# Cross-attention on one core: the query projection and the output projection change places within a TensorE step

## The reference, cut to what is computed

```python
q = split_heads(x @ Wq.T, 20)                 # x: 2 x 2048 x 640, 20 heads of 32
k = split_heads(ctx @ Wk.T, 20)               # ctx: 2 x 77 x 1024
v = split_heads(ctx @ Wv.T, 20)
probs = softmax(einsum('bhsd,bhld->bhsl', q, k) / sqrt(32), axis=-1)
out = merge_heads(einsum('bhsl,bhld->bhsd', probs, v))
return out @ Wo.T + bo + x
```

## Time and profile before

| | us |
|---|---|
| median of 3 runs | 434.07 (433.29 to 434.44) |
| the profiled execution | 434.35 |
| its span, first to last instruction | 432.6 |
| PE busy in it | 424.6 (98%) |
| ACT, POOL, DVE busy in it | 253.9, 301.0, 231.6 |

### The profile page before, as it was taken

The page is one execution under the profiler, slowest core; times in us unless marked ns, Lnnn a source line. Parts: engine busy times, 40 slices in busy tenths (PEclk is TensorE's granted clock), DMA queues, the critical chain, the costliest instruction groups (busy, mean ns, idle before and its releaser), DMA issues.

```text
span 432.6 us, 8258 instructions
## 1 busy us (share of the span) xinstructions
PE 424.6 (98%) x2538; PEld 310.7 (72%) x2538; DVE 231.6 (54%) x437; ACT 253.9 (59%) x509; POOL 301.0 (70%) x256
## 2 busy tenths in 40 slices
PE   8999989999999999999999999999999999999996
PEld 6877765577776777777777677777777767777775
DVE  0354785655555555555555555555555555555623
ACT  1638887757465755748464755757564755755510
POOL 8337798999658765969659674969659684865460
PEclk9999999999999999999999999999999999999999
DMA  8998536444454346543455335643355333444203
GB/s 280 353 327 266 210 110 220 150 149 145 137 197 157 134 156 204 192 146 125 145 184 184 124 131 205 205 168 124 124 192 192 128 122 137 156 159 161 76 24 121
DMA packets 39614, 72.68 MB, mean 168 GB/s; under 512 B 5024, under 2 KB 6176, under 8 KB 39584
## 3 DMA queue, kind: packets, MB, share of 16 engines
q1 hardware_dynamic: 28784, 52.62, 34.6%
q10 hardware_dynamic: 10800, 19.67, 14.1%
HBM read 28.81 MB, written 10.49 MB: 91 GB/s over the span
## 4 chain that ended last, share of the span: by engine, by line
PE 89%; DMA 3%; SPq 2%; ACT 2%; POOL 1%; DVE 1%; issue 1%; POOLq 0%; ACTq 0%
PE ps_q L672 30%; PE ps_o L672 27%; PE ps_s L734 10%; PE ps_pv L741 7%; PE ps_m L720 5%; PE ps_den L746 4%; PE ps_o L655 2%; DMA x_f<-in_x 2%; PE ps_m L787 1%; DMA q_packed<-mxT 1%; PE ps_m L725 1%; PE ps_q L787 1%; SPq L264 1%; DVE x_f L576 1%; PE ps_o L787 1%
## 5 line engine op out<-in xcount | busy, mean ns | idle before, releaser
L336 POOL TENSOR_TENSOR p_lo<-p_f,p_hi 77x512 f16<-77x512 f32 x160 | 183.9, 1168 | 99.7 <-ACT p_hi L430 97.3
L426 ACT ACTIVATE p_f<-ps_s 77x512 f32<-77x512 f32 x160 | 94.7, 592 | 45.7 <-PE ps_s L734 45.7
L546 DVE TENSOR_REDUCE mx<-ps_m 128x4 f32<-128x308 f32 x160 | 69.3, 475 | 54.8 <-PE ps_m L720 54.6
L430 ACT ACTIVATE p_hi<-ps_s 77x512 f16<-77x512 f32 x160 | 93.5, 584 | 2.8 <-PE ps_den L746 2.7
L539 DVE TENSOR_TENSOR q_lo<-ps_q,q_hi 128x512 fp32r<-128x512 f32 x40 | 27.7, 692 | 102.6 <-ACT q_hi L412 102.6
L672 PE MATMUL ps_q<-x_hi,wq_hi 128*128 128x512 f32 x200 | 79.5, 397 | 0.7 <-POOL x_lo L327 0.3
L672 PE MATMUL ps_q<-x_lo,wq_hi 128*128 128x512 f32 x200 | 78.2, 391 | 0.0
L672 PE MATMUL ps_q<-x_hi,wq_lo 128*128 128x512 f32 x200 | 78.2, 391 | 0.0
L672 PE MATMUL ps_o<-attn_hi,wo_hi 128*128 128x512 f32 x170 | 69.7, 410 | 0.6 <-POOL attn_lo L342 0.6
L672 PE MATMUL ps_o<-attn_hi,wo_lo 128*128 128x512 f32 x170 | 66.9, 393 | 0.0
L672 PE MATMUL ps_o<-attn_lo,wo_hi 128*128 128x512 f32 x170 | 66.8, 393 | 0.0
(11 more groups left out here) (105 smaller groups left out, 517.1 us busy)
## 6 DMA issues: line engine op xcount, KB each, us to landing
q_packed<-q_hi SPq DMA_DIRECT2D x80, 256.0 KB, 2.5
x_f<-in_x SPq DMA_DIRECT2D x40, 256.0 KB, 3.4
q_packed<-q_lo SPq DMA_DIRECT2D x40, 256.0 KB, 3.2
x_res<-in_x ACTq DMA_DIRECT2D x35, 256.0 KB, 2.7
out<-out_sb ACTq DMA_DIRECT2D x35, 256.0 KB, 2.6
wk_sb<-in_wk SPq DMA_DIRECT2D x8, 320.0 KB, 5.8
wv_sb<-in_wv SPq DMA_DIRECT2D x5, 512.0 KB, 5.9
wq_sb<-in_wq SPq DMA_DIRECT2D x5, 320.0 KB, 4.8
```

What stands on the lines that cost most here:

```text
L336: nc.gpsimd.tensor_tensor(p_lo[:, i, :], p_f[:, i, :], p_hi[:, i, :], ALU.subtract).then_inc(plo_done, 1)
L426: nc.scalar.activation(p_f[:, i, :], ps_s[i % 2][0:L, :], ACT.Exp, scale=SCALE).then_inc(pf_done, 1)
L430: nc.scalar.activation(p_hi[:, i, :], ps_s[i % 2][0:L, :], ACT.Exp, scale=SCALE).then_inc(phi_done, 1)
L546: nc.vector.tensor_reduce(mx[:, g % RS, :, tt], ps_m[tt % 2][:, 0:HG * L].rearrange("p (h k) -> p h k", k=L), AX_X, ALU.max).then_inc(max_ ...
```

## The change

In PE's steps the two projections change places: the query projection goes chunk by chunk into the places between maxima and scores, the output projection runs whole at the end. In steps that have no query projection left, (7, 3) and (7, 4), the output projection stays in the places. The filling steps are untouched, so 32 steps change, (1, 1) to (7, 2). On DVE q_low is issued ahead of finish_out. No instruction is added or removed.

```diff
@@ DVE, step
+                if exists(shift(t, g, 2)[0]):
+                    q_low(*shift(t, g, 2))
                 for tile in out_tiles(t, g):
                     finish_out(*tile)
-                if exists(shift(t, g, 2)[0]):
-                    q_low(*shift(t, g, 2))
@@ PE, step
-                if tiles:
-                    project_out(*tiles[0], (0, 1))
+                query = shift(t, g, 2)
+
+                def between(chunks):
+                    if exists(query[0]):
+                        project_q(*query, chunks)
+                    elif tiles:
+                        project_out(*tiles[0], chunks)
+
+                between((0, 1))
                 if exists(max_t):
                     max_scores(max_t, max_g, 2, batch(max_t))
                     max_scores(max_t, max_g, 3, batch(max_t))
                 if exists(t):
                     scores(t, g, 2, batch(t))
-                if tiles:
-                    project_out(*tiles[0], (2, 3))
+                between((2, 3))
                 if exists(t):
                     scores(t, g, 3, batch(t))
                 if exists(max_t):
                     transpose_max(max_t, max_g)
-                if tiles:
-                    project_out(*tiles[0], (4,))
-                if exists(shift(t, g, 2)[0]):
-                    project_q(*shift(t, g, 2), range(G))
+                between((4,))
+                if exists(query[0]) and tiles:
+                    project_out(*tiles[0], range(G))
```

## The result

The changed kernel takes 448.07 us (447.43 to 448.49, 4 runs) against 433.68 us before (433.10 to 434.44, 4 runs): ratio 1.0332, 95% interval 1.0316 to 1.0347. That is 14.4 us more; 15.3 were predicted, with 444.4 to 454.5 as the range.

The account below looks back on a forecast made before the run. PE's own instructions were taken to bound the kernel from step (1, 2) on. The profiled 434.35 us plus 15.8 (six blocks, 2.63 each) less 0.5 for step (1, 1) gave 449.6 us, range 444.4 to 454.5.

Parts of the forecast that it names:

- Steady steps cost nothing: In steady steps the swapped projections, new waits, DVE's order and transfers were to cost nothing.
- The transfers' collision: Rival: pack_q's transfer stretches load_max past 4.8 us, scores 0 wait 0.5 us in 32 steps, 466 us; chance 0.03.
- ACT's casts wait for output tile (t-2, 4): Steps (t, 0), t = 2 to 7: attn_high of chunks 0 and 1 waits until that tile has read them.
- Exponentials 2 3.77 us late: ACT in step (t, 0): exponentials 2 start 3.77 us late behind the waiting cast, and everything behind is as late.
- place 1: Start of step (t, 1): PE's `values` wait for ACT's last p_hi, 1.15 us late.
- place 2: Step (t, 1): the second part of `values` waits for POOL's last p_lo, 1.73 us late.
- place 3: Step (t, 1): scores 0 wait for load_max, the query projection for q_low, up to 1.9 us late.
- place 4: Step (t, 2): the second part of `values` waits for POOL's gapless attn_low and p_low chain, 2.63 us late in all.
- Step (1, 1) gains 0.5: Output projection no longer waits for attn_lo, about 1.2 us; a new p_lo wait leaves 0.5, bounds 0 and -1.8.
- the rival: Clock falls after PE's pauses: six steps take double, 509 us; chance 0.02.
- Only step (t, 1) pays: Rival: POOL has more room, only step (t, 1)'s waits remain, 1.7 to 1.9 us a block, 444.5 us; chance 0.06.
- Not slower: Rival: attn_high's wait in step (t, 0) is covered, only step (1, 1)'s gain remains, about 433.3 us; chance 0.03.

Follow-up runs that it names:

- experiment 1: Changed kernel with PE's and DVE's old order put back in the steps with g = 0 alone; 432.94 us, ratio 0.9994 to the kernel before.
- experiment 3: Changed kernel with ACT's five attn_high casts put last in its steps with g = 0, PE and DVE untouched; 433.17 us, ratio 1.0006.
- experiment 4: Changed kernel with POOL's attn_low of chunks 3 and 4 in blocks 1 to 6 cut to 64 of 512 columns; 444.46 us, ratio 1.0247.
- experiment 6: Changed kernel with five extra 16-column subtractions on POOL ahead of attn_low of chunk 4, blocks 1 to 6; 457.54 us, ratio 1.0517.
- experiment 7: As experiment 3, plus in step (1, 0) attn_high 0 and 1, q_high, attn_high 2 to 4, all behind exponentials 3; 432.28 us, ratio 0.9965.
- experiment 9: Kernel before the change with only experiment 7's new order in ACT's step (1, 0); 432.67 us, ratio 0.9985.
- experiment 10: The version of experiment 7 run once more, on the same chip as experiment 9; 432.26 us, ratio 0.9973.
- experiment 2: Changed kernel with the swap kept only in the steps with g = 0, all others as before; 452.52 us, ratio 1.0431.
- experiment 5: Changed kernel with DVE's old order, finish_out ahead of q_low, and PE as changed; 448.00 us, ratio 1.0332.
- experiment 8: As experiment 2 (swap only in steps with g = 0), but finish_out ahead of q_low everywhere; 451.20 us, ratio 1.0401.

## Why the prediction was right, point by point

- *Steady steps cost nothing.* Shown by experiment 1: of its 26 swapped steps none after (1, 2) is over 9.86 us. The transfers' collision did not come; load_max of the changed kernel landed after 1.8 to 4.3 us, below the 4.84 from which it would have counted:

```profile
DMA to landing us min/median/max: 1.8/2.8/4.3
```

- *ACT's casts wait for output tile (t-2, 4), in six blocks, and what stands behind them is late.* Shown by experiment 3, which keeps PE's order and takes that position away.
- *Exponentials 2 3.77 us late.* 3.71. But "everything behind is late as well" by the same amount was the mis-sized term: the last p_hi was 3.46 late, since ACT's old pause for the transpose took up 0.25. That carries through: place 1 was 0.83 us late and not 1.15 (179.94), place 2 1.42 and not 1.73 (181.19), place 3 1.58 and not 1.9 (182.69; hardly more than place 2, because scores 0 follow `values` by 0.54 us as before and only q_low adds 0.16), place 4 2.35 and not 2.63 (191.94, which is 22.67 us after the block's first step began, where before it was 20.32). Six times 0.28 is 1.7 us too much in the sum.
- *Place 4 is the largest and contains the others.* Shown from both sides, by experiments 4 and 6.
- *Step (1, 1) gains 0.5.* 0.52 in the profile; experiment 1 has the gain alone, 0.3 us with an interval that reaches 0.
- *The steps that the profile would show.* The sum of a block's three long steps was nearly right (32.0 us against 31.8), its split wasn't: (t, 0) was to stay at 9.84 us, (t, 1) and (t, 2) to take 11.7 and 10.5, and they took 10.67, 10.71 and 10.44. The pause of place 1 stands ahead of the `values` of (t, 1) and so falls into (t, 0) when steps are counted from start to start. Likewise "all others 9.82" left out (1, 2), which took 10.48: the prediction's own new wait for p_lo, which makes a gain of 0.5 out of one of 1.2 in step (1, 1), is in it. Taken word for word, its sign of being wrong ("if steps other than these grow") would have counted (t, 0) and (1, 2) against it.
- *The clock.* The forecast's sum had none of it, and the rival gave a whole step at half pace after each pause. Neither is what happened: in the changed kernel's profile one block of six has a fall. In experiment 6 three of six have one. The one fall cost 0.7 us net. So the sum of 15.3 should have been 15.3 - 1.7 + 0.7 = 14.3, against 14.4 between the medians. That the two errors pull in opposite ways is luck. The absolute forecast, 449.6 us against 448.07, is off by another 0.7 because it started from the profiled execution's 434.35 and not from the median, 433.68.
- *The rivals.* "Only step (t, 1) pays" was 1.7 us a block, and it is what experiment 4 shows once POOL's chain is cut. "Not slower" needs the wait to be covered; experiment 3 gets there in another way, by leaving nobody behind it.

## What to carry to other kernels

When a consumer of a shared buffer is moved later, look for the producer that overwrites this buffer and read what stands behind it in its engine's queue: here the cost was in that queue, not at the buffer. If nothing needs the overwriting soon, try it last; here that made the late read free. Size the delay at the last instruction of the chain and not at the first, since idle time in between takes up some, and find the chain with no idle time at all, since that one hands the delay on whole.

## What the runs showed of the hardware

The granted clock of TensorE fell although no pause of PE in the steps was longer than 0.8 us. In the changed kernel's timeline, block 4:

```profile
231.38 0.40 PE L741 MATMUL ps_pv<-p_hi,v_hi 77*32 77x512 f16 x4 [0.75 <-ACT p_hi L430]
...
232.63 0.40 PE L741 MATMUL ps_pv<-p_lo,v_hi 77*32 77x512 f16 x4 [0.42 <-POOL p_lo L336]
...
235.15 0.63 PE L672 MATMUL ps_q<-x_lo,wq_hi 128*128 128x512 f32 x1
235.58 0.63 PE L672 MATMUL ps_q<-x_hi,wq_hi 128*128 128x512 f32 x1
...
237.57 0.40 PE L672 MATMUL ps_q<-x_hi,wq_hi 128*128 128x512 f32 x1
237.80 0.39 PE L672 MATMUL ps_q<-x_hi,wq_lo 128*128 128x512 f32 x1
```

After two pauses in step (4, 1) the matmuls start 0.43 us apart and not 0.23, which is 1.2 GHz and not 2.4, until about 237; then the pace is back. The window of that step:

```profile
231.38:243.50 12.12, 11.70 (x59) 8.23 (x60) 6.01 (x11) 6.79 (x14) 11.89 (x11) 0.86 0.65 216
```

It lasts 12.12 us at a mean clock of 0.86, 1.4 more than the 10.67 to 10.71 of the other five (t, 1), which had the same two pauses. So a fall follows the same pauses in some blocks and not in others. Half of the 1.4 us came back at once: step (4, 2) took 9.81 us in place of 10.5, because PE, being later, no longer met POOL's chain. In experiments 1, 3, 7, 9 and 10 and in the kernel before, without such pauses from (1, 3) on, no step from there to (7, 4) shows a fall. The kernels with six blocks of pauses show one in the changed kernel, two in experiment 2, none in experiment 4, one each in experiments 5 and 8, three in experiment 6, each time in the step of the pauses. In experiment 2 one of the two windows (14.07 us, mean clock 0.76) has a fall about twice as long.

What a fall costs differs: 1.4 us in the window of the changed kernel, 1.55 in experiment 6, but 0.43 and 0.26 in windows (t, 1) of experiments 2 and 8 (12.26 and 12.10 against 11.83 and 11.84), where PE at full pace waits for attn_lo. That this wait hides the fall is a reading of the windows; no run tests it.

The Trainium skill (TensorE: Matmul & The Clock Gate, "A second HAM failure mode: psum-queue depth-cycling") tells of another kernel in which small pauses between groups of matmuls made the clock go up and down. The traces agree in kind, with one block of six in the changed kernel and three of six in experiment 6, there all in steps with the pause of about 1.33 us and none in (t, 1), where the pauses were as in the changed kernel. What decides whether a given pause does it stays open.
